# Reordering the work where the stages of a four-layer attention and FFN kernel meet

## The chip, the cores and the metric

The kernel runs on one core of one Trainium2 chip. The metric is the device time of one execution in microseconds (us). Three executions of the kernel before took 1570.99, 1571.07 and 1574.42 us; their median is 1571.07 us.

## The reference

The residual stream `x` is 1024 tokens of 512 numbers. Each of four layers adds an attention of the normalised `x` over a context of 1024 tokens, and then an FFN of the normalised `x`:

```python
x = x + _L0_xattn_ref(_layernorm(x), ctx, Wq, Wk, Wv, Wo)     # 32 heads of 128, 4 KV heads
x = x + _L0_ffn_ref(_layernorm(x), base_W, gate_W, lora_A, lora_B)   # dense + top 2 of 28 experts of rank 8
x = x + _L1_xattn_ref(_layernorm(x), ctx, mask, ...)           # 32 heads, 8 KV heads, RMS norm of q and k
x = x + _L1_ffn_ref(_layernorm(x), W_base, gate_W, A, B)       # dense + top 2 of 8 experts of rank 8
x = x + _L2_xattn_ref(...); x = x + _L2_ffn_ref(...); x = x + _L3_xattn_ref(...); x = x + _L3_ffn_ref(...)
```

The change touches the start, the first two attentions and the first two FFNs. Layers 2 and 3 keep their code.

## The kernel before

**Tiles.** `x` stays in SBUF as 8 tiles of 128 tokens. Every product in float32 is made of three products (`PASSES`) of rounded "high" parts and "low" remainders: ScalarE (ACT) copies a PSUM bank to the high part, and VectorE (DVE) subtracts that from the bank for the low part. For weights, which come by DMA from the SP queue into `stage_q`, `stage_o` and `stage_kv`, the low part of some 512-wide slices is made by GpSimd (POOL, `low`, L488) and of others by VectorE (`low_wq`, L1721).

**Order.** Nothing is scheduled at run time. Each engine works through its own list in the order of the code, and waits on semaphores. So an instruction that waits holds up all behind it on its engine.

**An attention** is a pipeline of 64 steps (8 head groups by 8 tiles). In `attention` of TensorE (L737) step `t` holds the q product of step t+1 (first attention, `q_unit`) or t (second, `q_proj`), the transposes of the probabilities of step t-2 (`p_transpose`, L840), the scores of step t-1 (L759), the output product of step t-3 (`out_proj`, L869, bank psY) and the product with V of step t-2 (`attend`, L850). VectorE's list for a step (L1847 on) holds the layer norm `xn` (`ln_norm`), the low part of the transposed probabilities (`pT_lo`), the row maxima (`row_max`), the low part of q, the division by the sum (`normalise`), the residual addition (`x_add`), the low part of the attended values (`oT_lo`) and the statistics of a finished tile (`last_stats`).

**Where stages meet.** The steps from 60 on (`LN_SLOT`) finish the residual tiles one by one, and each such step also transposes one normalised tile for the FFN (`ln_transpose`, L706; its low part, `ln_lo`, on VectorE). The transposes use the bank psP (psT for tile 7), which the probabilities' transposes use too: `p_transpose(63)` waits until the low part of tile 4 has been read out. Steps 63 and 64 have no q product. Behind the loop an epilogue drains the last steps with `dense_product` 0 and 1 of the FFN among them.

**The FFN** (`ffn_step`, L975 and L2045) makes for each tile a gate product (L720, bank psQ), on VectorE the choice of two experts (`gates`, L1770, which ends in the hidden values `s_sb`), a transpose of those (`hidden_transpose`, L955), the dense product (L733) and the experts' product (L971), the last two in one of three banks (`ring3`). The weights of the experts' product are cut into parts (`high_b`, `low_b`) once the last output product of the attention is done. `hidden_transpose(0)` waits for the low part of tile 6, and tile 7 of the norm is transposed behind `dense_product(2)`.

**The second attention's head.** Its step 0 holds the q product of tile 0, the norm transpose of tile 6, the k and v product (`kv_proj`, L812), the norm transpose of tile 7, the q product of tile 1, and the transposes of q and k; step 1 the k and v product, the scores of step 0, the q product of tile 2 and the transposes. VectorE's step 0 has the low part of tile 7 ahead of `qk_normalise(0)`, which makes `q_sb` (L1892) from a reciprocal root (`rms`) of POOL.

**The start.** SP issues tiles 0 and 1 of `x`, four slices of the first q weights, then the context (1 MB), the first k and v weights (0.5 MB) and the other six tiles of `x` (1.5 MB). POOL makes low parts of two q slices, of two context slices and of the k and v weights, and only then the reciprocal roots of tiles 2 on; VectorE has its share of the context's low parts ahead of the statistics of tile 2.

## Time and profile before

| | us |
|---|---|
| profiled execution, whole | 1570.53 |
| its span, first to last instruction | 1568.7 |
| median of three timed executions | 1571.07 |
| TensorE matmuls busy (PE) | 1501.3 (96%) |
| weight loads busy (PEld) | 1323.4 (84%) |
| VectorE busy (DVE) | 1008.9 (64%) |
| ScalarE busy (ACT) | 821.1 (52%) |
| GpSimd busy (POOL) | 379.4 (24%) |

The span is what lies between the first and the last instruction. Matmuls overlap, so the difference between the starts of two groups tells the time that the first holds TensorE better than its length does. The mean granted TensorE clock was 0.985 of full speed.

### The profile page before, as it was taken

Reading aid. Unit: us, or ns where it says so; the run is one execution under the profiler, and the core shown is the slowest. Engines: PE = TensorE matmul, PEld = TensorE weight load, DVE = VectorE, ACT = ScalarE, POOL = GpSimd, SP = SyncE. Lnnn points to the kernel's source line nnn. Section 1 sums busy time; section 2 is a strip of 40 time slices with the busy share of each in tenths; the row PEclk is TensorE's granted clock in tenths of the full one; section 3 lists DMA queues with packets and bytes.
Section 4 is the critical chain, followed back from the end, with each engine's and each line's share of the span. In section 5 each row is a group of like instructions: output and inputs, shape, how many; then the busy total and the mean of one; then the engine's idle time right before and its main releaser. Section 6 shows DMA issues by size and latency. Waiting matters only on the chain.

```text
span 1568.7 us, 27791 instructions
## 1 busy us (share of the span) xinstructions
PE 1501.3 (96%) x9658; PEld 1323.4 (84%) x9658; DVE 1008.9 (64%) x2475; ACT 821.1 (52%) x2862; POOL 379.4 (24%) x388
## 2 busy tenths in 40 slices
PE   7999999999999998999999999999999998879896
PEld 7899999999999997788888888888888887667785
DVE  6666556655665568766665666656666677688775
ACT  4556445644555455346565556555565652554542
POOL 4102010201111011133232332323232321543420
PEclk9999999999999999999999999999999998799998
DMA  4100100100011001010101010101100001111001
GB/s 182 62 28 28 42 28 28 56 14 28 28 55 36 33 13 41 28 41 28 41 28 41 28 50 19 68 8 62 41 28 32 5 8 55 44 55 35 24 11 57
DMA packets 14624, 60.21 MB, mean 38 GB/s; under 512 B 2085, under 2 KB 3493, under 8 KB 9497
## 3 DMA queue, kind: packets, MB, share of 16 engines
q1 hardware_dynamic: 14488, 58.46, 10.5%
q8 instruction: 79, 1.29, 0.4%
q14 instruction: 57, 0.46, 0.1%
HBM read 56.36 MB, written 2.10 MB: 37 GB/s over the span
## 4 chain that ended last, share of the span: by engine, by line
PE 59%; issue 27%; DVE 7%; POOL 3%; ACT 2%; DMA 1%; POOLq 0%; DVEq 0%; SPq 0%; ACTq 0%
PE psY L869 15%; PE psQ L790 11%; PE psKV L812 8%; PE psSO L759 3%; PE psSO L856 2%; PE psTP L822 2%; PE psQ L775 2%; PE psTP L775 2%; PE psSO L760 2%; POOL wo L488 1%; PE psTP L840 1%; PE psKV L733 1%; PE psQ L1137 1%; PE psQ L720 1%; PE psTP L706 1%
## 5 line engine op out<-in xcount | busy, mean ns | idle before, releaser
L869 PE MATMUL psY<-wo,oT 128*128 128x512 f32 x1536 | 384.9, 399 | 1.8 <-DVE oT L1721 1.2
L869 PEld LDWEIGHTS psY<-wo,oT 128*128 128x128 f32 x1536 | 278.6, 188 | 65.8 <-POOL wo L488 2.2
L488 POOL TENSOR_TENSOR wo<-stage_o,wo 128x512 fp32r<-128x512 f32 (+2 forms) x71 | 91.1, 1309 | 309.0 <-ACT wo L1275 309.0
L1275 ACT ACTIVATE pT<-psTP 128x512 fp32r<-128x512 f32 (+1 forms) x128 | 62.8, 491 | 169.4 <-PE psTP L840 169.4
L593 POOL TENSOR_TENSOR rms<-ms_eps,minus_half 128x5 f32<-128x5 f32 x64 | 74.7, 1168 | 280.2 <-DVE ms_eps L1884 277.2
L1356 ACT ACTIVATE prob<-wide,neg_mx 128x128 f32<-128x128 f32 x256 | 99.8, 391 | 75.0 <-DVE neg_mx L1871 74.8
L1353 ACT ACTIVATE prob<-s_sb,neg_mx 128x64 f32<-128x64 f32 x256 | 86.0, 337 | 98.3 <-DVE neg_mx L1871 98.3
L1721 DVE TENSOR_TENSOR pT<-psTP,pT 128x512 fp32r<-128x512 f32 (+1 forms) x128 | 71.3, 557 | 77.4 <-ACT pT L1275 76.4
L1721 DVE TENSOR_TENSOR v<-psKV,v 128x128 fp32r<-128x128 f32 x64 | 18.7, 292 | 140.4 <-ACT v L1275 140.4
L812 PEld LDWEIGHTS psKV<-wkv,arena 128*128 128x128 f32 x768 | 99.8, 190 | 9.0 <-DVE kT L1908 4.6
L812 PE MATMUL psKV<-wkv,arena 128*128 128x256 f32 x768 | 103.4, 284 | 1.2 <-DVE kT L1908 1.2
L790 PE MATMUL psQ<-wq,hT 128*128 128x512 f32 x384 | 104.0, 408 | 0.0
L775 PE MATMUL psQ<-hT,wq 128*128 128x256 f32 x768 | 99.6, 285 | 4.2 <-DVE hT L1721 2.9
L790 PE MATMUL psQ<-hT 128*128 128x512 f32 x372 | 100.1, 407 | 0.0
L775 PEld LDWEIGHTS psQ<-hT,wq 128*128 128x128 f32 x768 | 94.9, 192 | 5.9 <-DVE hT L1721 3.1
L812 PE MATMUL psKV<-wkv,hT 128*128 128x256 f32 x768 | 99.8, 286 | 0.0
L775 PE MATMUL psTP<-hT,wq 128*128 128x256 f32 x768 | 99.1, 286 | 0.0
L1275 ACT ACTIVATE oT<-psSO 128x512 fp32r<-128x512 f32 (+1 forms) x132 | 76.4, 579 | 38.8 <-PE psY L869 32.1
L775 PEld LDWEIGHTS psTP<-hT,wq 128*128 128x128 f32 x768 | 96.0, 195 | 0.0
L812 PEld LDWEIGHTS psKV<-wkv,hT 128*128 128x128 f32 x768 | 94.1, 192 | 0.3
L1326 ACT ACTIVATE pT<-psQ 128x128 fp32r<-128x128 f32 x252 | 66.3, 280 | 53.4 <-PE psQ L790 53.4
L1721 DVE TENSOR_TENSOR oT<-psSO,oT 128x512 fp32r<-128x512 f32 (+1 forms) x132 | 88.7, 672 | 7.5 <-ACT oT L1275 7.2
(303 smaller groups left out, 3389.5 us busy)
## 6 DMA issues: line engine op xcount, KB each, us to landing
stage_o<-in_wo SPq DMA_DIRECT2D x16, 1024.0 KB, 4.8
stage_q<-in_wq SPq DMA_DIRECT2D x15, 1024.0 KB, 5.3
stage_kv<-in_wkv SPq DMA_DIRECT2D x12, 512.0 KB, 3.6
stage_q<-in_ctx SPq DMA_DIRECT2D x16, 256.0 KB, 2.8
stage_o<-in_ctxT SPq DMA_DIRECT2D x2, 1024.0 KB, 5.8
stage_q<-in_base SPq DMA_DIRECT2D x2, 1024.0 KB, 4.9
out<-x_res SPq DMA_DIRECT2D x8, 256.0 KB, 2.4
x_res<-in_x SPq DMA_DIRECT2D x1, 1536.0 KB, 11.1
```

The lines of the kernel that those rows point to most:

```text
L488: g.tensor_tensor(dst[LO], stage, dst[HI].bitcast(f32), ALU.subtract).then_inc(ld[done or what + "_lo"], 1)
L593: g.tensor_tensor(rms[:, t.res(2)], ms_eps[:, t.res(2)], minus_half[:, 0:5], ALU.pow).then_inc(s["rms"], 1)
L759: mm(bank[:, at:at + 2 * keys], q_of(HI), k_of(slice(0, 2)), start=True, stop=False)
L775: m = mm(out, wq[:, wl, c, head], lat_pair(xl, c, k.res(NT) // 2), start=c == 0 and i == 0, stop=c == KT - 1 and i == 2)
L790: m = mm(by_eight(q_bank(st)[:]), lat(xl, k, n), wq_slice(st.div(NT) + a.wq0, wl, k), start=k == 0 and i == 0, stop=k == KT - 1 and i == 2)
L812: m = mm(psKV[:, b * 256:(b + 1) * 256], lhsT, wkv_k(wl, k, 256), start=k == 0 and i == 0, stop=k == KT - 1 and i == 2)
L869: m = mm(psY[:], oT[:, ol, h, :], wo[:, wl, h, :], start=h == 0 and i == 0, stop=h == HQ - 1 and i == 2)
L1275: copy = lambda o, i: nc.scalar.activation(o, i, ACT.Copy)
L1326: i = nc.scalar.activation(junk_q[h], q_bank(st)[:, h * HD:(h + 1) * HD], ACT.Square, accum_out=ssq[:, n, h:h + 1])
L1353: e = nc.scalar.activation(prob[:, at], s_sb[:, at], ACT.Exp, bias=neg_mx[:, j:j + 1], scale=1.0, accum_out=sums[:, j:j + 1])
L1356: e = nc.scalar.activation(prob[:, at], wide[:, at], ACT.Exp, bias=neg_mx[:, j:j + 1], scale=a.scale, accum_out=sums[:, j:j + 1])
L1721: return V.tensor_tensor(dst_lo, src, dst_hi.bitcast(f32), ALU.subtract)
```

## The change

It moves instructions in the lists of all engines and gives two FFN products other banks. The core of the diff:

```diff
@@ ring3: banks of the dense products
-        return (psS, psKV, psY)[n % 3]
+        return (psKV, psS, psY)[n % 3]
@@ sync: loads at the start
         sp.wait_ge(ld["x1"], 16)
+        sp.dma_start(x[:, 2:4], io["x"][:, 2:4]).then_inc(ld["x23"], 16)
         sp.dma_start(stage_o[:], io["ctxT"][0]).then_inc(ld["ctx_in"], 16)
         sp.dma_start(stage_kv[:], io["wkv0"][0]).then_inc(ld["wkv_in"], 16)
-        sp.dma_start(x[:, 2:NT], io["x"][:, 2:NT]).then_inc(ld["x_rest"], 16)
+        sp.dma_start(x[:, 4:NT], io["x"][:, 4:NT]).then_inc(ld["x_rest"], 16)
@@ gpsimd
         low_wq(0)
+        low("wq", halves(wq, 2), stage_q[:, 2], 3, "wq_lo_v")
         low_ctx(0)
...
             ln_rstd(1, n)
-            if n == 3:
+            if n == 2:
                 low_wq(8)
@@ tensor: scores(u)
+                if a.index == 1 and u.t == 0:
+                    pe.wait_ge(FS["x_add"], NT)
@@ tensor: kv_proj
-                    pe.wait_ge(FS["x_add"], NT)
+                    pe.wait_ge(FS["x_add"], NT - 1)
@@ tensor: attention, the loop over steps
                             q_proj(t, 2, 4)
+                        if t.t == 0:
+                            experts(FF[0], NT - 1)
+                        if t.t == 1:
+                            q_proj(t.back(-1), 0, 4)
                         kv_proj(t)
...
                     if t1.exists and not units:
                         scores(t1)
-                        if not t.exists:
+                        if t.exists:
                             gate_product(f, 0)
+                        else:
+                            dense_product(f, 0)
...
-                if a.norm_slot(t) == "between":
+                if a.rms and a.norm_slot(t) == "between":
                     ln_transpose(next_ln, t.t - LN_SLOT, ...)
                 if a.rms and t2.exists and t.exists:
                     attend(t2)
+                if a.rms and not t.exists:
+                    gate_product(f, 0)
                 if t3.exists:
                     out_proj(t3, 0, 4)
+                if not a.rms and a.norm_slot(t) == "between":
+                    ln_transpose(next_ln, t.t - LN_SLOT, ...)
                 if a.rms and not t.exists:
                     scores(t1)
+                    dense_product(f, 0)
                     attend(t2)
...
                 if a.index == 1 and t.static and t.t == 0:
+                    q_proj(t.back(-1), 0, 4)
                     ln_transpose(2, NT - 1, ...)
                 if t.exists and a.rms:
-                    if t.t < 2:
-                        q_proj(t.back(-1), 0, 4)
                     q_transpose(t)
                     k_transpose(t)
@@ tensor: attention, the epilogue
-            if a.rms:
-                gate_product(f, 0)
-            pe.wait_ge(s["max"], last.c + 1)
-            dense_product(f, 0)
             p_transpose(last)
             out_proj(before, 0, 4)
             attend(last)
+            pe.wait_ge(s["max"], last.c + 1)
+            dense_product(f, 1)
             ln_transpose(next_ln, 5, ...)
-            dense_product(f, 1)
+            gate_product(f, 1)
             out_proj(last, 0, 4)
             ln_transpose(next_ln, 6, ...)
@@ tensor: ffn_step
-            if t == 1:
-                gate_product(f, t)
...
             if t < NT:
+                if t == 1:
+                    ln_transpose(f.ln, NT - 1, lambda: None)
                 if t > 1:
                     gate_product(f, t)
-                if t == 1:
-                    pe.wait_ge(A["x_add"], (f.index + 1) * STEPS)
-                    dense_product(f, 2)
-                    ln_transpose(f.ln, NT - 1, lambda: None)
-                if t > 2:
+                    if t == 2:
+                        pe.wait_ge(A["x_add"], (f.index + 1) * STEPS)
                     dense_product(f, t)
-            if 0 <= u < NT:
+            if 0 <= u < NT - (f.index == 0):
                 experts(f, u)
@@ scalar: first attention, steps 60 on
-                    ln_hi(next_ln, t.t - LN_SLOT)   # ahead of exps(t1)
+                    ln_hi(next_ln, t.t - LN_SLOT)   # behind exps(t1)
-                    next_wq(t)   # step 62, ahead of exps
+                if not a.rms and t.t == STEPS - 2:
+                    next_wq(t)   # step 62, behind oT_hi
-            pT_hi(last)
             gate_exp(FF[a.index], 0)
+            pT_hi(last)
@@ vector: attention
                 if scores_first:
+                    pT_lo(t2)
                     row_max(t1)
                 if a.norm_slot(t):
                     ln_norm(next_ln, t.t - LN_SLOT)
-                if t2.exists:
+                if t2.exists and not scores_first:
                     pT_lo(t2)
...
-                if a.norm_slot(t) == "between":
+                if a.rms and a.norm_slot(t) == "between":
                     ln_lo(next_ln, t.t - LN_SLOT)
...
                     x_add(t3)
+                if not a.rms and a.norm_slot(t) == "between":
+                    ln_lo(next_ln, t.t - LN_SLOT)
...
+                if not a.rms and t.t == STEPS - 2:
+                    low_wq(8)   # was ahead of normalise(t1)
@@ vector: the epilogue and the start
-            pT_lo(last)
             gates(FF[a.index], 0)
             ln_norm(next_ln, 5)
+            pT_lo(last)
...
-        low_wq(0, 2)
         ln_lo(0, 0)
```

## Rows read from the trace of the kernel before

**Rows 1.** The page: the chain of work that ended last, by engine.

```profile
PE 59%; issue 27%; DVE 7%; POOL 3%; ACT 2%; DMA 1%; POOLq 0%; DVEq 0%; SPq 0%; ACTq 0%
```

**Rows 2.** TensorE's waits over the span: releaser, total us, times, longest.

```profile
PE psTP L955 <- DVE s_sb L1778: 4.7, 4, 2.6
...
PE psTP L706 <- DVE pT L1721: 2.3, 3, 1.0
```

**Rows 3.** Windows: stretch, length, busy us by engine, PEclk, DMA share, GB/s.

```profile
10.00:12.00 2.00, 0.01 (x1) 0.01 (x1) 1.94 (x4) 0.99 (x3) 0.09 (x1) 1.00 1.07 447
641.00:660.00 19.00, 16.91 (x102) 14.20 (x101) 15.45 (x52) 8.90 (x17) 4.34 (x5) 1.00 0.15 56
1313.00:1321.00 8.00, 7.60 (x25) 6.44 (x25) 4.64 (x22) 0.63 (x3) 0.81 (x2) 0.50 0.00 1
```

**Rows 4.** Timeline of the start: start, length, engine, line, operation, idle before.

```profile
14.87 2.93 POOL L488 TENSOR_TENSOR wkv<-stage_kv,wkv 128x512 fp32r<-128x512 f32 x2
...
18.96 1.12 PE L706 MATMUL psTP<-ident,xn 128*128 128x128 f32 x4 [3.82 <-DVE xn L1762]
```

**Rows 5.** Timeline of VectorE, one round of the first attention's last steps.

```profile
596.24 0.55 DVE L1762 TENSOR_SCALAR xn<-x_res,mv,rstd 128x512 f32<-128x512 f32 x1 [0.67 <-POOL rstd L501]
...
605.27 0.55 DVE L1762 TENSOR_SCALAR xn<-x_res,mv,rstd 128x512 f32<-128x512 f32 x1 [0.66 <-POOL rstd L501]
```

**Rows 6.** Timeline of TensorE, from step 63 to the last transposes.

```profile
619.00 0.98 PE L850 MATMUL psSO<-pT,arena 128*128 128x256 f32 x6 [1.97 <-DVE pT L1721]
...
626.85 3.00 PE L733 MATMUL psSO<-wq,hT 128*128 128x512 f32 x12
629.69 0.60 PE L840 MATMUL psTP<-ident,prob 128*128 128x128 f32 x4
```

**Rows 7.** Timeline of VectorE, step 64 and the gates behind it.

```profile
622.90 0.69 DVE L1858 TENSOR_TENSOR wide<-psSO,wide 128x512 f32<-128x512 f32 x1
...
626.44 0.69 DVE L1877 TENSOR_TENSOR prob<-prob,rsums 128x512 f32<-128x512 f32 x1
...
631.56 0.18 DVE L1819 MAX8 top<-psQ 128x8 f32<-128x28 f32 x1
...
633.66 0.54 DVE L1762 TENSOR_SCALAR xn<-x_res,mv,rstd 128x512 f32<-128x512 f32 x1
```

**Rows 8.** Timeline of all engines behind the first attention's last product.

```profile
637.51 2.89 PE L869 MATMUL psY<-wo,oT 128*128 128x512 f32 x12
...
640.43 0.69 DVE L1926 TENSOR_TENSOR x_res<-x_res,psY 128x512 f32<-128x512 f32 x1 [2.82 <-PE psY L869]
...
642.85 2.72 POOL L488 TENSOR_TENSOR wo<-stage_o,wo 112x512 fp32r<-112x512 f32 x2
...
642.92 1.50 DVE L1762 TENSOR_SCALAR xn<-x_res,mv,rstd 128x512 f32<-128x512 f32 x1
```

**Rows 9.** Timeline of all engines, head of the second attention.

```profile
693.53 0.68 DVE L1892 TENSOR_TENSOR q_sb<-psQ,rms 128x512 f32<-128x512 f32 x1
...
696.41 1.69 PE L812 MATMUL psKV<-wkv,arena 128*128 128x256 f32 x12 [0.84 <-DVE kT L1908]
...
700.43 0.69 DVE L1892 TENSOR_TENSOR q_sb<-psY,rms 128x512 f32<-128x512 f32 x1
```

**Rows 10.** Timeline of all engines, end of the second attention and its FFN.

```profile
1283.75 0.22 PE L759 MATMUL psSO<-kT,qT 128*128 128x128 f32 x1
...
1289.57 0.68 DVE L1721 TENSOR_TENSOR hT<-psTP,hT 128x512 fp32r<-128x512 f32 x1
...
1290.39 0.41 PE L840 MATMUL psTP<-ident,prob 128*128 128x128 f32 x2 [0.45 <-DVE hT L1721]
...
1303.71 1.50 DVE L1762 TENSOR_SCALAR xn<-x_res,mv,rstd 128x512 f32<-128x512 f32 x1
...
1313.40 0.42 PE L955 MATMUL psTP<-ident,s_sb 128*64 128x128 f32 x1 [2.61 <-DVE s_sb L1778]
...
1316.06 5.42 PE L733 MATMUL psSO<-hT 128*128 128x512 f32 x12
```

More of the change, by code:

```diff
@@ L697, in wq_split @@
         def wq_split(load, k):
-            pe.wait_ge(ld["wq_lo" if k < 2 else "wq_lo_v"], load * 2 + (k % 2 + 1))
+            pe.wait_ge(ld["wq_lo" if k < 2 else "wq_lo_v"], load * 2 + (2 if load == 0 and k > 1 else k % 2 + 1))
         def ln_transpose(ln, n, free):
@@ L916, in attention @@
                     attend(t2)
+                if a.rms and not t.exists:
+                    gate_product(f, 0)
                 if t3.exists:
                     out_proj(t3, 0, 4)
+                if not a.rms and a.norm_slot(t) == "between":
+                    ln_transpose(next_ln, t.t - LN_SLOT, lambda: ln_bank_free(next_ln, t.t - LN_SLOT, t2))
                 if a.rms and not t.exists:
                     scores(t1)
+                    dense_product(f, 0)
                     attend(t2)
@@ L1434, in attention @@
                     next_wq1(t)
-                if t.exists and not a.rms and not early and t.res(8) == 6:
+                if t.exists and not a.rms and not early and t.res(8) == 6 and t.t < LN_SLOT:
                     next_wq(t)
@@ L1472, in attention @@
             last = Step(STEPS - 1, STEPS, done=a.done)
+            gate_exp(FF[a.index], 0)
             pT_hi(last)
-            gate_exp(FF[a.index], 0)
             oT_hi(last)
@@ L1747, in x_stats @@
         def x_stats(n):
-            dve.wait_ge(ld[f"x{n}" if n < 2 else "x_rest"], 16)
+            dve.wait_ge(ld[f"x{n}" if n < 2 else "x23" if n < 4 else "x_rest"], 16)
             ln_stats(0, n)
@@ L1973, in attention @@
                     ln_lo(0, n)
-                if a.norm_slot(t) == "between":
+                if a.rms and a.norm_slot(t) == "between":
                     ln_lo(next_ln, t.t - LN_SLOT)
@@ L1979, in attention @@
                     qk_normalise(t)
-                if t.exists and not a.rms and t.res(8) == 6:
+                if t.exists and not a.rms and t.res(8) == 6 and t.t < LN_SLOT:
                     low_wq(t.div(8) + 1)
@@ L1985, in attention @@
                     x_add(t3)
+                if not a.rms and a.norm_slot(t) == "between":
+                    ln_lo(next_ln, t.t - LN_SLOT)
                 if t2.exists and a.rms:
```

## The prediction

> **What bounds the kernel now.** The chain that ended last, on the page, gives 59% of the span to TensorE's matmuls and 27% to its own issue, 7% to VectorE [rows 1]. So TensorE's list is the time, plus the places where it waits. TensorE's waits say where: no large group stands there, only single waits of 0.4 to 3.8 us; the hidden values of the FFNs, for example, cost 4.7 us in four waits [rows 2]. The timelines of those places then show who is late: nearly always VectorE, at a point of its list where several short results are due one after another. The windows add one thing. From 1313 to 1321 us, in the second FFN, TensorE has half its clock (PEclk 0.50, 1.2 instead of 2.4 GHz), while the same stretch of the first FFN has all of it [rows 3].
>
> All differences below are starts minus starts. A q or dense product holds TensorE for 2.8 us (626.85 to 629.69 [rows 6]), and so does an output product; gate 1.5, scores 1.0, a group of four transposes 0.4, attend 0.7. A copy or subtraction of 512 columns takes 0.6 on ACT and 0.68 on VectorE.
>
> **The start: +1.2.** Tiles 2 and 3 arrive sooner, but their statistics stand in VectorE's list behind the context's low parts, and their root stands in POOL's list behind the low part of the k and v weights: that ends at 14.87 + 2.93 = 17.80, and root, normalising and transposes follow, these at 18.96, after 3.82 us without work for TensorE [rows 4]. The 0.52 MB now ahead of the context cost it 0.52 MB / 447 GB/s = 1.2 us [rows 3]; POOL's context slices, its weights, the root and the transposes go with it. The first q product may start up to 0.6 us sooner, as VectorE loses a slice to POOL, but it only ends in the longer wait. Bounds: 0 (the context is late for nobody) to +2.5 (the third slice delays POOL too). I take 1.2.
>
> **The first attention, steps 60 to 63: -1.3.** Norm transposes no longer wait in front of the output product (2.3 us in three waits [rows 2]). But VectorE goes round its list in 605.27 - 596.24 = 9.03 us per step [rows 5], and TensorE needs only 8.1 (2.9 + 0.4 + 1.0 + 2.8 + 0.4 + 0.7). In the round of before, the low part of the norm (0.68 [rows 10]) lies in the time in which VectorE waits for the exponentials; now it stands behind `x_add` and adds 0.6 to the round, of which some 0.4 comes back from a wait for ACT. At about 9.2 per round the wait moves to the transposes of the probabilities and is not gone: 0. In step 63 the weight slices stand no longer ahead of the exponentials and the division, which have been waiting behind them; the gate product fills the wait for the probabilities (0.9), and `attend`'s wait (1.97 [rows 6]) shrinks, though VectorE now has the two slices right ahead of `pT_lo(61)`. I take -1.3, bounds -5.7 (all the waits of these steps) and 0.
>
> **Step 64 and the epilogue: +4.1.** This is the largest term. From the start of scores(63), new list: scores 1.0, dense product 2.8, then transposes 62, done at 4.4; ACT's copy to 5.0; VectorE's `pT_lo(62)`, which now stands ahead of `row_max(63)`, to 5.7. The row maxima start only then. From their start to the end of the division it is 626.44 + 0.69 - 622.90 = 4.2 us [rows 7]: probabilities at 10.0. Then `x_add` 0.6, `oT_lo` 0.6, and the low part of tile 4 until 11.9. TensorE has done output product 61, attend 62 and transpose 4 by 8.2, and the next in its list is `p_transpose(63)`, which needs both: a wait of 3.7, where before the dense product stood in that place and the transposes started at 629.69 with no wait [rows 6]. Then output product 62 until 15.1; VectorE has statistics (1.0), `gates(0)` and the norm of tile 5 (631.56 to 633.66 and 0.5 [rows 7]), and only then `pT_lo(63)`: ready about 16.1, a wait of 0.9 for `attend(63)`, against 0.5 that goes. 3.7 + 0.4 = 4.1; bounds 2 and 5.
>
> **Behind the last output product: +2.0.** Before, tile 7's normalised values were ready at 642.92 + 1.50 = 644.42, which is 4.2 after the end of the output product's place (637.51 + 2.7), and POOL's expert weights at 642.85 + 2.72 = 645.57, 5.4 after it [rows 8]. Both hang on that product (through `x_add` at 640.43 and ACT), and the new list keeps their order. Between stood gate 1 (1.5) and dense 2 (2.8); now only transposes of 1.0 in all stand ahead of `experts(0)`: 4.4 us of waits, and 0.3 for the next hidden values. In exchange 0.9 goes here and, as dense 2 now stands before `experts(1)`, the 1.8 us of waits at the third hidden transpose. 4.7 - 2.7 = 2.0; bounds 0.5 and 3.5.
>
> One rule bears on this place. The normalising took 1.50 with POOL's subtraction running, against 0.55 alone [rows 5, 8]. The Trainium skill (GPSIMD Engine Reference, Key points) says that POOL shares its SBUF interfaces with VectorE and contends with instructions in a two-port mode or with two SBUF inputs; trace and rule agree. By it the collision comes back in the new order and is now paid by TensorE; if it didn't, the term would be 1.0 smaller.
>
> **Head of the second attention: +2.5.** The expert product of tile 7 behind the q product removes a wait of 0.7. But q product 1 now stands before tile 7's transposes, and VectorE has that tile's low part ahead of `q_sb(0)`: transposes, copy, low part and `q_sb` follow one another (0.6 + 0.7 + 0.7 + 0.7) with nothing left for TensorE, a wait of 2.3; `q_sb(0)`, at 693.53 before [rows 9], comes at about 695. Then q product 2 fills the 0.84 before the k product of step 1, but it is gone from where it covered the other chain: from that k product to `q_sb(1)` ready it is 700.43 + 0.69 - 696.41 = 4.7 us [rows 9], with only 1.5 + 0.8 of work now, a wait of 2.4. The probabilities of step 0 are then late by 1 too. Sum of waits 8.0 against 5.5. Bounds 1 and 3.5.
>
> **Second attention's end and FFN: +2.2 at equal clock.** The same steps. From scores(63) to tile 4's low part it is 1289.57 + 0.68 - 1283.75 = 6.5 [rows 10]; with gate and output product ahead scores start 0.4 later, at 1284.1, so the transposes of the probabilities start at about 1290.7 against 1290.39 before [rows 10], gate and dense product done in both: +0.3. `pT_lo(63)` behind `gates(0)` adds 0.5. Behind the last output product the normalised tile 7 comes late as in the first FFN (1.50 again, 1303.71 [rows 10]), and `gates(1)`, 0.7 longer here than the 2.1 of the first FFN, stands behind it, without gate 1 and dense 2 to cover either: +4.0. The wait of 2.61 at the third hidden transpose goes [rows 10]: net +2.2. Bounds 0 and 4.
>
> **The clock: +3.** In the second FFN half clock made 12 products last 5.42 instead of 3.0 and the gate 1.3 more: 3.8 us [rows 3, 6, 10], after TensorE had worked little for some 5 us. The new order works 1.0 in 5.4 us there in both FFNs. So I take the second FFN as slow as before (0) and the first one, whose clock was 1.00 [rows 3], falling too, with 3.0 for a gate, a dense and an expert product. Bounds -3.8 and +4.5. The Trainium skill (TensorE: Matmul & The Clock Gate, HAM oscillation) says that idle gaps send the engine back to half clock, and every gap costs anew; by it the fall comes wherever the new waits stand, which is the +3; the rival without it stands below.
>
> **Sum.** 1.2 - 1.3 + 4.1 + 2.0 + 2.5 + 2.2 + 3.0 = 13.7. On the profiled execution's 1570.53 (span 1568.7 and 1.8 around it) that is 1584.2; the median shown is 0.5 above that execution. Own range 1578 to 1590.
>
> **Rivals.**
> - *The waits, without the clock.* The first FFN keeps full clock: 1581.2; if the second does too, 3.8 less, 1577.4. For it: step 63 of before waited 3.4 us in 7 and kept 1.00. Against: there longer products stood between. 0.17.
> - *The products fill what they were moved into.* VectorE's results depend on inputs rather than on its list, so gate 0, dense 0 and dense 2 cover the waits of 3.4 in step 63, 1.8 and 2.6 in the FFNs, the half clock (3.8) goes with the last, and nothing new is due: 1570.5 + 1.2 - 11.6 = 1560. It decides at `p_transpose(63)`: if it starts within 1 us of the transposes before it, this holds. Against it: `pT_lo(62)` stands ahead of the row maxima in the new list. 0.13.
> - *Gains and waits cancel.* Steps 60 to 63 give 4 to 5 us instead of 1.3, the head of the second attention nothing, and the clock does as now: 1584.2 - 3 - 2.5 - 3 - 3 = 1573, or two or three lower. 0.15.
>
> **How the numbers follow.** Forecast 0.55, the rivals 0.17, 0.13, 0.15. What a measurement here can tell from no change is 0.3%, 4.7 us: faster is below 1566.4, slower above 1575.8. Faster holds the filling rival, 0.13; within 0.3%, two thirds of the cancelling one, 0.10; slower the rest, 0.77. The range 1567 to 1590 leaves out the filling rival and the worst of the bounds.
>
> **What would show it.** Right: VectorE's rounds in steps 60 to 62 still 9 us or more; 3 us or more of wait before `p_transpose(63)` in the first attention and 2 in the second; TensorE working 1 us in the 5 behind each last output product; PEclk 0.50 in the first FFN; a wait of 2 us before each of the first two q transposes; norm transposes at 20.2 at the start. Wrong: the FFN's first gate started no later than before relative to the work done, or PEclk 1.00 in both FFNs.

## The result and the profile after

The changed kernel takes 1588.12 us (median of four executions, 1585.94 to 1588.55), 17.0 more than the 1571.12 of the kernel before beside it: ratio 1.0108, 95% interval 1.0083 to 1.0118. Its profiled execution took 1588.29 us, with a span of 1586.6 and a mean granted clock of 0.975 (before: 1570.53, 1568.7 and 0.985). The prediction was 1584.2, range 1567 to 1590.

TensorE's waits that are new or have grown [rows 2], then four windows [rows 3]:

```profile
PE psTP L827 <- DVE q_sb L1906: 5.9, 3, 2.3
PE psTP L845 <- DVE hT L1735: 5.8, 3, 3.4
PE psTP L968 <- DVE hT L1735: 4.2, 2, 2.1
```

```profile
641.00:660.00 19.00, 15.24 (x69) 12.54 (x68) 12.19 (x36) 6.34 (x12) 3.75 (x4) 0.82 0.16 56
1320.00:1336.00 16.00, 13.93 (x54) 10.66 (x55) 10.78 (x44) 2.13 (x8) 2.35 (x4) 0.68 0.39 132
700.00:720.00 20.00, 14.10 (x78) 12.08 (x76) 8.72 (x24) 7.25 (x36) 3.08 (x3) 0.83 0.00 2
598.55:607.30 8.75, 8.61 (x61) 7.82 (x60) 6.79 (x14) 4.57 (x15) 0.55 (x1) 1.00 0.20 60
```

The low part of a norm (`hT`), the normalised values and `q_sb` are waited for, all from VectorE; and three stretches run with PEclk (the granted clock as a share of full speed) at 0.82, 0.68 and 0.83. The first of them had 1.00 before. The last row is one round of VectorE: 8.75 us, in which it works for 6.79. The same round before [rows 5]:

```profile
596.24:605.27 9.03, 8.39 (x62) 7.77 (x60) 6.98 (x14) 4.53 (x13) 0.55 (x1) 1.00 0.18 58
```

TensorE's timeline: the transposes of the probabilities, one group per round, then from the norm transposes of step 64 on [rows 6, 8].

```profile
588.59 0.60 PE L845 MATMUL psTP<-ident,prob 128*128 128x128 f32 x4
...
596.73 0.60 PE L845 MATMUL psTP<-ident,prob 128*128 128x128 f32 x4
...
605.18 0.63 PE L845 MATMUL psTP<-ident,prob 128*128 128x128 f32 x4
...
613.93 0.63 PE L845 MATMUL psTP<-ident,prob 128*128 128x128 f32 x4 [0.73 <-DVE hT L1735]
...
627.72 0.66 PE L708 MATMUL psTP<-ident,xn 128*128 128x128 f32 x4
631.76 0.63 PE L845 MATMUL psTP<-ident,prob 128*128 128x128 f32 x4 [3.39 <-DVE hT L1735]
632.15 4.58 PE L874 MATMUL psY<-wo,oT 128*128 128x512 f32 x12
636.57 0.88 PE L855 MATMUL psSO<-pT,arena 128*128 128x256 f32 x6
...
647.29 0.43 PE L968 MATMUL psTP<-ident,s_sb 128*112 128x128 f32 x2 [2.08 <-DVE hT L1735]
648.85 0.66 PE L708 MATMUL psTP<-ident,xn 128*128 128x128 f32 x4 [1.13 <-DVE xn L1776]
650.06 2.90 PE L984 MATMUL psKV<-wo,oT 112*128 112x512 f32 x6 [0.56 <-POOL wo L489]
...
653.04 2.91 PE L722 MATMUL psQ<-wkv,hT 128*128 128x252 f32 x12
```

The rounds are 8.14, 8.45 and 8.75, the last with a wait of 0.73: TensorE runs ahead of VectorE, whose rounds are 8.88 and 8.75, until it has caught up with it. Later the transposes of the last probabilities wait 3.39 with everything that could cover them done, and the output product behind them holds TensorE for 636.57 - 632.15 = 4.42 instead of 2.8: half clock. Behind the last output product come waits of 2.08, 1.13 and 0.56, and an expert product and a gate product that hold TensorE 2.7 each instead of 1.5.

The head of the second attention, and the end of it with its FFN [rows 9, 10]:

```profile
703.21 0.66 PE L827 MATMUL psTP<-ident,q_sb 128*128 128x128 f32 x4 [2.01 <-DVE q_sb L1906]
...
703.73 4.59 PE L795 MATMUL psQ<-hT 128*128 128x512 f32 x12
...
712.81 0.66 PE L827 MATMUL psTP<-ident,q_sb 128*128 128x128 f32 x4 [2.26 <-DVE q_sb L1906]
...
1305.08 0.66 PE L845 MATMUL psTP<-ident,prob 128*128 128x128 f32 x2 [1.70 <-DVE hT L1735]
1305.39 4.42 PE L874 MATMUL psY<-wo,oT 128*128 128x512 f32 x12
...
1327.57 5.20 PE L735 MATMUL psY<-hT 128*128 128x512 f32 x12
```

Both q transposes wait over 2 us, and q product 2 (4.43 to the next) runs mostly at half clock.

To see where the 17.9 us between the spans arise, I cut each trace at six instructions: the transposes of the probabilities of steps 60 and 65 (P60, P65) in the first attention, the last hidden transpose of its FFN (H), the first output product of the second attention (O), its last transposes of probabilities (Q), and the last hidden transpose of the second FFN (G). Each column is a difference of two starts. The kernels below the second row are explained in the sections that follow:

| kernel | start to P60 | P60 to P65 | P65 to H | H to O | O to Q | Q to G | G to end | span |
|---|---|---|---|---|---|---|---|---|
| before | 586.6 | 43.1 | 53.9 | 31.4 | 575.4 | 53.5 | 224.8 | 1568.7 |
| after | 588.6 | 43.2 | 59.4 | 37.7 | 576.2 | 55.3 | 226.2 | 1586.6 |
| start_back | 585.5 | 43.2 | 58.0 | 36.1 | 576.2 | 55.3 | 226.3 | 1580.6 |
| head_back | 586.5 | 43.2 | 59.3 | 31.4 | 576.3 | 54.9 | 229.3 | 1580.9 |
| behind_back | 587.6 | 43.2 | 54.8 | 36.2 | 576.2 | 53.7 | 227.6 | 1579.2 |
| step64_back | 588.6 | 43.6 | 57.7 | 36.2 | 576.3 | 55.4 | 226.2 | 1583.9 |
| fillers | 588.0 | 43.2 | 58.6 | 33.7 | 577.4 | 53.1 | 226.1 | 1580.1 |
| tile4_psT | 588.9 | 41.3 | 60.8 | 36.1 | 574.2 | 57.1 | 226.2 | 1584.7 |
| best1 | 586.1 | 41.3 | 54.0 | 32.5 | 575.4 | 53.0 | 227.9 | 1570.2 |
| best2 | 586.3 | 41.3 | 54.0 | 31.4 | 575.6 | 54.0 | 227.7 | 1570.3 |
| before_fill | 586.4 | 43.1 | 53.8 | 33.0 | 575.5 | 49.9 | 227.6 | 1569.2 |
| best3 | 584.9 | 41.4 | 54.0 | 33.0 | 575.5 | 51.7 | 228.2 | 1568.7 |
| fillers2 | 588.5 | 43.2 | 56.2 | 33.7 | 576.2 | 54.9 | 224.8 | 1577.5 |
| best4 | 586.9 | 41.3 | 54.0 | 32.4 | 575.4 | 49.0 | 226.2 | 1565.2 |

The first and the last column scatter among kernels with the same code there (G to end: 224.8 to 229.3), the others by some tenths where no clock falls. Where it falls they scatter too: with the new head of the second attention H to O is 37.7 in the changed kernel's trace, but 36.1 or 36.2 in start_back, behind_back, step64_back and tile4_psT, whose code there is the same. So a column says more than a median where 1 or 2 us are asked for, but a single trace can be 1.6 us off in a stretch that has half clock.

### The profile page after: what moved, and what is told of

Same layout as the page of the kernel before. It is cut to its first block, busy times and chain, and to the rows that moved or that the text cites. A ratio compares the mean times of both kernels' runs of the same rounds, so it can differ in the third digit from the quotient of the medians.

```text
span 1586.6 us, 27793 instructions
## 1 busy us (share of the span) xinstructions
PE 1515.3 (96%) x9658; PEld 1333.8 (84%) x9658; DVE 1006.4 (63%) x2474; ACT 820.8 (52%) x2862; POOL 381.0 (24%) x389
## 4 chain that ended last, share of the span: by engine, by line
PE 60%; issue 26%; DVE 7%; POOL 4%; ACT 2%; DMA 1%; POOLq 0%; DVEq 0%; SPq 0%; ACTq 0%
PE psY L874 15%; PE psQ L795 11%; PE psKV L817 8%; PE psSO L764 3%; PE psSO L861 2%; PE psTP L827 2%; POOL wo L489 2%; PE psSO L765 2%; PE psQ L780 1%; PE psTP L845 1%; PE psQ L722 1%; PE psTP L780 1%; PE psSO L735 1%; PE psQ L1147 1%; PE psKV L1191 1%
## 5 line engine op out<-in xcount | busy, mean ns | idle before, releaser
L795 PE MATMUL psQ<-hT 128*128 128x512 f32 x372 | 103.3, 417 | 0.0
L1285 ACT ACTIVATE oT<-psSO 128x512 fp32r<-128x512 f32 (+1 forms) x132 | 76.4, 579 | 40.7 <-PE psY L874 32.4
L489 POOL TENSOR_TENSOR wq<-stage_q,wq 128x512 fp32r<-128x512 f32 x35 | 44.8, 1291 | 205.3 <-ACT wq L1285 166.6
```

What stands on the lines that cost most here:

```text
L489: g.tensor_tensor(dst[LO], stage, dst[HI].bitcast(f32), ALU.subtract).then_inc(ld[done or what + "_lo"], 1)
L795: m = mm(by_eight(q_bank(st)[:]), lat(xl, k, n), wq_slice(st.div(NT) + a.wq0, wl, k), start=k == 0 and i == 0, stop=k == KT - 1 and i == 2)
L1285: copy = lambda o, i: nc.scalar.activation(o, i, ACT.Copy)
```

## Undoing one part at a time

Theory: the order leaves TensorE with nothing to do at four places, and each wait costs its length and the half clock behind it. The rival: the waits are the whole of it. Each kernel undoes one part; its median stands against the kernel before on the same chip, and "less" is against the 17.0 of the changed kernel.

**start_back** gives the start its old order (x 2 to 7 behind the context, weight slice 2 on VectorE):

```diff
-        sp.dma_start(x[:, 2:4], io["x"][:, 2:4]).then_inc(ld["x23"], 16)
         sp.dma_start(stage_o[:], io["ctxT"][0]).then_inc(ld["ctx_in"], 16)
```

> The new kernel with the start as before: tiles 2 to 7 of x behind the context, VectorE makes the low part of weight slice 2. Theory (the second load of x delays the context and with it POOL's chain, 1.2 by the prediction, 1.7 to 2.0 by the position of the probabilities' transposes in the two traces): 1588.1 - 1.9 = 1586.2, and those transposes of step 58 at 586.6 again instead of 588.6. Rival (the start's delay is swallowed by later waits): 1588.1, those transposes still near 588.6.

Measured: 1584.98 (1582.43 to 1590.24), 13.9 above before, ratio 1.0097 (1.0079 to 1.0114): about 3 less than the 17.0. P60 at 585.5. The four traces with the old start and nothing added there (before, this one, best1, best2) have P60 at 585.5 to 586.6, the six with the new one (after, head_back, behind_back, step64_back, fillers, tile4_psT) at 586.5 to 588.9; the means are 586.1 and 588.0. The theory holds with 1.9, though the two groups touch (586.5 and 586.6); of the 3 in the median the rest is within its scatter. The start of the new kernel shows the chain:

```profile
17.35 2.94 POOL L489 TENSOR_TENSOR wkv<-stage_kv,wkv 128x512 fp32r<-128x512 f32 x2
...
21.44 1.01 PE L708 MATMUL psTP<-ident,xn 128*128 128x128 f32 x4 [3.08 <-DVE xn L1776]
```

POOL's low parts of the k and v weights start at 17.35 instead of 14.87, and the norm transposes follow at 21.44 instead of 18.96 [rows 4]. With the old start back the transposes are at 19.80, 1.6 sooner. Two things were undone together here, but the traces tell them apart: ACT's first copy of the context, which waits for the transfer, starts at 13.71 in the changed kernel and at 12.06 in start_back, and POOL has waited 2.69 us for ACT when it comes to its context slices. The late context is the cause, not the third weight slice on POOL.

**head_back** undoes the head of the second attention:

```diff
-                        if t.t == 0:
-                            experts(FF[0], NT - 1)
-                        if t.t == 1:
-                            q_proj(t.back(-1), 0, 4)
...
-                    q_proj(t.back(-1), 0, 4)
                     ln_transpose(2, NT - 1, ...)
+                    if t.t < 2:
+                        q_proj(t.back(-1), 0, 4)
                     q_transpose(t)
```

> The new kernel with the head of the second attention as before (expert product of tile 7 in the FFN's own place, q products 1 and 2 ahead of the q transposes). From the FFN's last hidden transpose to output product 4 the two traces differ by 6.3 us. Theory (two waits of 2 us ahead of the q transposes and a third, and TensorE's clock falling to half because of them): 6.3 less, 1581.8, and PEclk near 1.00 from 700 to 720. Rival (the clock falls there by itself, only the waits are due to the order): 2.5 less as predicted, 1585.6, PEclk still near 0.7.

Measured: 1582.66 (1581.49 to 1583.04), 11.6 above before, ratio 1.0072: 5.4 less. H to O is 31.4, exactly as before, against 37.7, and the clock is 1.00 from 700 to 740. TensorE's timeline, the q transposes of steps 0 and 1, with no idle time noted before them:

```profile
700.29 0.60 PE L824 MATMUL psTP<-ident,q_sb 128*128 128x128 f32 x4
...
707.04 0.60 PE L824 MATMUL psTP<-ident,q_sb 128*128 128x128 f32 x4
```

Neither waits. The theory holds, the rival (only 2.5, half clock all the same) falls.

**behind_back** gives gate 1, dense 2 and tile 7's transposes their old order at the head of both FFNs:

```diff
-            gate_product(f, 1)
             out_proj(last, 0, 4)
...
+            if t == 1:
+                gate_product(f, t)
...
+                    dense_product(f, 2)
                     ln_transpose(f.ln, NT - 1, lambda: None)
```

> The new kernel with gate 1, dense 2 and the norm transposes of tile 7 at the head of the two FFNs in their old order, in the new banks. Theory (what covered the late normalised tile 7 and POOL's expert weights is back): first FFN 2.2 of waits and 2.8 of half clock less, second FFN 2.5 less with the wait of 2.6 and the half clock of before back at the third hidden transpose: 7.5 less, 1580.6, PEclk 1.00 in the first FFN. Rival (the clock falls in the first FFN because of the half clock at step 64 just before, or by itself): 4.7 less, 1583.4, PEclk 0.50 somewhere from 640 to 660.

Measured: 1581.29 (1580.34 to 1583.54), 10.3 above before, ratio 1.0068: 6.7 less, between the theory's 7.5 and the rival's 4.7. P65 to H is 54.8 (4.6 less), Q to G 53.7 (1.6 less); the trace also has 1.6 less in the head of the second attention, which this edit doesn't touch. The window of the first FFN:

```profile
641.00:660.00 19.00, 16.91 (x99) 14.13 (x99) 15.68 (x52) 8.31 (x15) 4.33 (x5) 1.00 0.15 56
```

Full clock with the same busy time as before, although the output product behind the last transposes, some 10 us ahead, still ran at half clock (4.42 to the next). So the fall behind the last output product comes from the waits there and not from the one before.

**step64_back** puts dense product 0 back ahead of the transposes of the last probabilities:

```diff
-                        else:
-                            dense_product(f, 0)
...
+            dense_product(f, 0)
             p_transpose(last)
```

> The new kernel with dense product 0 of both FFNs back ahead of the transposes of the last probabilities (VectorE's and ACT's orders stay new). Theory (those transposes wait 3.4 us for tile 4's low part because the product that covered them was moved ahead): the wait is at most 0.5 and the output product behind it has full clock: in the first attention 3.4 + 1.6 less, in the second 1.7 + 1.5 less: 1588.1 - 8 = 1580. Rival (VectorE's order, pT_lo ahead of the row maxima, is the cause; without the dense product in step 64 the chain of scores, maxima and division is only moved forward with TensorE): the wait moves to attend(63) or stays above 2, and 1585 or more remains.

Measured: 1585.06 (1584.33 to 1586.99), 14.0 above before, ratio 1.009: 3 less, not 8. TensorE's timeline, the transposes of steps 64 and 65 with their output products:

```profile
623.61 1.09 PE L845 MATMUL psTP<-ident,prob 128*128 128x128 f32 x4 [2.52 <-DVE hT L1733]
624.35 4.03 PE L874 MATMUL psY<-wo,oT 128*128 128x512 f32 x12
...
632.15 0.63 PE L845 MATMUL psTP<-ident,prob 128*128 128x128 f32 x4
632.53 2.97 PE L874 MATMUL psY<-wo,oT 128*128 128x512 f32 x12
```

The wait of 3.39 is gone and its output product has full clock (2.97), but the transposes of step 64, which dense 0 had covered, now wait 2.52, and the output product behind those runs at half clock (4.03). There is one product for two holes. The theory fails; the rival has the time (1585 or more) and a wait above 2, though the wait moved to the transposes of step 64. Of the 3 less in the median the trace puts only 1.3 into the first attention's end and its FFN (43.6 and 57.7 against 43.2 and 59.4); 1.5 lies in the head of the second attention, whose code is untouched. In the second attention nothing was gained (O to Q 576.3, Q to G 55.4): its transposes still wait, 1.79 us, for the low part of tile 4. Moving dense 0 alone was the wrong cure there too.

## Is it the clock?

**fillers** leaves the order and puts idle products into the waits, the identity times itself, whose result nobody reads (each stands in the timeline as two matmuls, so 14 are x28):

```diff
+            filler(psT, 14)          # mm(bank, ident, ident), 14 times
             p_transpose(last)
...
+                    if t.t < 2:
+                        filler(psO[:, 0], 8)
                     q_transpose(t)
```

> The new kernel with idle products of the identity in the places where TensorE waits, into banks free there: 14 ahead of the transposes of the last probabilities, 8 ahead of the first hidden transpose, 4 ahead of the norm transposes of tile 7, 8 ahead of each of the first two q transposes; nothing else moved. Theory (the waits themselves, by leaving TensorE idle, cost the half clock behind them; half clock costs 1.6 + 2.8 + 3.8 in the first FFN's surroundings and the head of the second attention and 1.5 + 3.8 in the second): the same waits stay in time but PEclk is 1.00 behind them: 8 to 12 less, 1576 to 1580. Rival (the clock falls for another reason, or the fillers delay the work that they stand ahead of): 1588 or up to 2 more, PEclk 0.50 in the same places.

Measured: 1581.94 (1579.04 to 1585.41), 11.2 above before, ratio 1.007 (1.0055 to 1.0085): 6 less. TensorE's timeline, step 65, then the head of the second attention:

```profile
627.67 3.29 PE L705 MATMUL psTP<-ident 128*128 128x128 f32 x28
631.24 0.63 PE L849 MATMUL psTP<-ident,prob 128*128 128x128 f32 x4 [0.28 <-DVE hT L1745]
631.62 3.00 PE L878 MATMUL psY<-wo,oT 128*128 128x512 f32 x12
635.32 0.98 PE L859 MATMUL psSO<-pT,arena 128*128 128x256 f32 x6 [0.70 <-DVE pT L1745]
...
646.14 3.54 PE L705 MATMUL psTP<-ident 128*128 128x128 f32 x16 [2.08 <-DVE hT L1745]
```

```profile
699.72 1.95 PE L705 MATMUL psSO<-ident 128*128 128x128 f32 x16
701.89 0.66 PE L831 MATMUL psTP<-ident,q_sb 128*128 128x128 f32 x4 [0.22 <-DVE q_sb L1916]
...
702.41 2.98 PE L799 MATMUL psQ<-hT 128*128 128x512 f32 x12
```

The transposes come when they came (631.24 after a start 0.5 sooner), but the output product takes 3.00 instead of 4.58. q product 2 takes 2.98 instead of 4.59, but that proves nothing: it took 2.98 to 3.01 in start_back, behind_back, step64_back and tile4_psT too, behind the same unfilled wait of 2.01. What tells is the k and v product behind the wait of 2.26: 1.70 here, 2.76 to 2.93 in all five traces with that wait unfilled. H to O falls from 37.7 to 33.7: of the head's 6.3 over the 31.4 of before, 4.0 was half clock (2.5 in the four other traces of this head) and 2.3 its waits. One group was set wrongly: the eight at 646.14 stand behind the wait of 2.08 instead of in it, run mostly at half clock and hold TensorE for 3.3 us. And the 14 stand in the second attention too, where they last longer than the wait of 1.70: O to Q is 1.2 longer. The theory holds here in kind, the size is short of its 8 to 12.

**before_fill** and **fillers2** do this with both orders, the second with the fillers now ahead of that wait, so that the two can be compared with the clock held:

> The kernel before with nothing moved, but idle products of the identity in the places of its longest waits: 11 more ahead of the first q product and 8 behind it at the start, 7 ahead of the second q transpose of the second attention, 10 ahead of the third hidden transpose of the second FFN, and 5, 12, 6 and 14 in the waits of the stage behind it. Theory (idle stretches cost the half clock that follows them, whatever the work is): of about 14 us that TensorE's work lasts longer at half clock in the trace of before (16 to 24, 1308 to 1323, 1348 to 1368, 1408 to 1416, 1536 to 1540 us) some 10 come back: 1561. Rival (the fillers delay the work and the clock falls elsewhere instead): 1569 to 1573.

> The new kernel with the idle products of before_fill at the start and behind the second FFN, and in its own waits: 14 and 7 ahead of the transposes of the last probabilities, 8 ahead of the first hidden transposes, 4 ahead of tile 7's norm transposes, 8 ahead of the first two q transposes, none longer than the wait. Theory (of the 17 us between the two kernels 8 to 9 are waits and the rest is half clock behind them): 8 to 9 more than before_fill, about 1570; PEclk 1.00 at 632, 652, 704 to 720 and 1320 to 1332 us. Rival (the waits are the whole of it and the clock only a companion): 15 or more above before_fill.

Measured: 1571.68 (1570.82 to 1573.3), 1.4 above before, ratio 1.0009 (1.0 to 1.0018), and 1580.82 (1578.4 to 1581.15), 10.5 above before, ratio 1.0063 (1.005 to 1.0077). The difference between the two orders is 9.1, as the theory had it; without fillers it is 17.0. Without the 1.5 us that before_fill loses to fillers of its own (below) it would be 10.6, so of the 17.0 some 9 to 11 are waits and the rest half clock. The clock is not held everywhere: in the second FFN of fillers2 one dense product still takes 4.59. But before_fill itself gained nothing, 1561 was expected, and the traces say why. Q to G fell from 53.5 to 49.9: the half clock of the second FFN was worth 3.7. The fillers ahead of the second q transpose, where the kernel before waits for nothing (its wait of 1.71 for `q_sb` is at the third), cost 1.5 (H to O). Behind the second FFN full clock did bring time, but one group of fillers took it again. Windows of that stage, the kernel before, then before_fill:

```profile
1348.00:1370.00 22.00, 17.41 (x92) 16.22 (x92) 11.75 (x28) 11.63 (x27) 12.40 (x16) 0.61 0.23 70
```

```profile
1346.00:1368.00 22.00, 18.30 (x148) 16.86 (x147) 14.12 (x35) 13.59 (x32) 13.24 (x19) 1.00 0.22 71
```

PEclk went from 0.61 to 1.00, and yet from G to the next hidden transpose it is 38.5 us in one and 38.7 in the other. The first gate product of that stage shows what happened between, again before, then before_fill (G is at 1343.9 and 1341.6):

```profile
1376.65 1.66 PE L720 MATMUL psSO<-wkv,hT 128*128 128x256 f32 x12
```

```profile
1371.70 3.29 PE L703 MATMUL psKV<-ident 128*128 128x128 f32 x28
1374.75 1.65 PE L724 MATMUL psSO<-wkv,hT 128*128 128x256 f32 x12
```

The gate product comes 32.7 us behind G before, with no wait ahead of it. In before_fill TensorE has reached that place 30.1 us behind G, 2.7 sooner, but there it has 14 idle products to do, which hold it for 3.0, and the gate product comes at 33.1. So half clock cost 2.7 us in this stage as well; the rival, that fillers delay the work, is what made before_fill no faster. best3 and fillers2 hold the same 14 products. No run left out only these.

## Towards a better kernel

**tile4_psT** gives the norm transposes of tile 4 the bank psT, so that the last probabilities don't wait for its low part:

```diff
-            return psT if n == NT - 1 and ln != 7 else psP
+            return psT if n == NT - 1 and ln != 7 or n == 4 and ln in (1, 3) else psP
```

> The new kernel with the norm transposes of tile 4 in the bank psT in both attentions, so that the transposes of the last probabilities no longer wait for that tile's low part; order unchanged. Theory (the wait of 3.4 us is made half by the shared bank: division done at 629.8, the low part of tile 4 at 631.6): transposes at 629.9 instead of 631.8 after the same start, the wait 1.6; 1.0 to 1.3 of it comes back before attend(63), whose low part stands behind gates(0); with the clock behind a shorter wait staying up, 2 to 4 less in all: 1584 to 1586. Rival (the chain scores, maxima, division alone is the wait): nothing, 1588.

Measured: 1591.31 (1585.81 to 1592.02), 20.5 above before, ratio 1.0123: a miss; 3 more than the changed kernel instead of 2 to 4 less.

```profile
630.18 0.66 PE L846 MATMUL psTP<-ident,prob 128*128 128x128 f32 x4 [1.51 <-DVE prob L1892]
631.38 3.02 PE L875 MATMUL psY<-wo,oT 128*128 128x512 f32 x12 [0.54 <-DVE oT L1736]
636.16 0.98 PE L856 MATMUL psSO<-pT,arena 128*128 128x256 f32 x6 [1.75 <-DVE pT L1736]
636.97 4.50 PE L735 MATMUL psSO<-wq,hT 128*128 128x512 f32 x12
```

The bank was half of the wait, as said (P60 to P65 1.9 less), but 1.4 of it comes back by H: 0.54 for the attended values of step 62 (`oT`), 1.75 for `pT_lo(63)` behind `gates(0)`, and then the half clock, which only moved to the dense product (4.50). The profiled execution is one of the two short ones of five (1586.51, span 1.9 less than the changed kernel's); why the other three took 1591 to 1592 no trace shows.

**best1** takes the kernel before with steps 60 to 64 of the first attention new, tile 4 in psT, and `pT_lo(63)` ahead of the gates:

```diff
+            pT_lo(last)
             gates(FF[a.index], 0)
             ln_norm(next_ln, 5)
-            pT_lo(last)
```

> The kernel before with only the steps 60 to 64 of the first attention new: norm transposes behind the output product, gate product 0 in step 63, dense product 0 in step 64, the weight slices behind the attended values of step 62; tile 4's norm in psT; pT_lo(63) ahead of the gates; start, heads, FFNs and the second attention as before. Theory (steps 60 to 63 gain 3.7, the wait ahead of the last probabilities' transposes is 1.6 to 1.9 instead of 0): 1.8 less than the kernel before, 1569.2. Rival (the clock falls behind that wait as in the new kernel, or the second FFN's chance moves): 0 to 2 more than the kernel before, 1571 to 1573.

Measured: 1572.05 (1570.57 to 1573.6), ratio 1.0006 (0.9998 to 1.0015). P60 to P65 is 41.3, the gain of 1.8 is there, and `attend(63)` waits no more; it is given back by the head (32.5) and the last stages (227.9), whose code is that of before. In the head the third q transpose waits 1.71 in both, and PEclk falls behind it in best1 and not in before. The median shows no gain: the rival's case.

**best2** also splits dense product 2 of the second FFN:

```diff
-                    dense_product(f, 2)
+                    dense_product(f, 2, 0, 2)
...
+                if t == 2 and f.index == 1:
+                    dense_product(f, 2, 2, KT)
```

> As the one before, and in the second FFN the second half of dense product 2 stands behind the gate product, ahead of expert product 1, instead of both halves together. Theory (the half clock of the second FFN comes from the wait of 2.3 to 2.6 at the third hidden transpose; split in two waits of about 1.3, it keeps full clock): 3.8 less than the one before, 1565.4, PEclk 1.00 throughout the second FFN. Rival (the waits are only divided and the clock falls all the same, since the work between them is as little): 1569.

Measured: 1571.61 (1567.78 to 1573.82), ratio 1.0001. Q to G is 54.0, 1.0 more than in best1: the rival's half clock, 3 us above its time. One wait of 1.49 is left, and TensorE has half clock from the gate product behind it (2.65 instead of 1.50) to the end of dense product 3:

```profile
1305.66 0.30 PE L961 MATMUL psTP<-ident,s_sb 128*64 128x128 f32 x1 [1.49 <-DVE s_sb L1790]
...
1315.27 4.97 PE L733 MATMUL psKV<-hT 128*128 128x512 f32 x12
```

**best3** is best1 with all fillers of before_fill:

> The first attention's steps 60 to 64 new as in best1, and the idle products of before_fill. Theory: best1 was 2.1 less than before up to the end of the first FFN and gave it back to half clock later; with the clock held the 2 are kept: 2 less than before_fill, 1559. Rival (VectorE is the bound there and the 2 us are lost at the next wait): the same as before_fill.

Measured: 1569.47 (1565.73 to 1573.22), ratio 0.9993 (0.9983 to 1.0003): not told from before, 2.2 below before_fill: the 2 us are kept, as the theory had it, but not the time of 1559. Here the clock fell twice in the second FFN, once among the fillers and once where none stand:

```profile
1308.25 4.06 PE L703 MATMUL psTP<-ident 128*128 128x128 f32 x20
...
1333.66 0.30 PE L967 MATMUL psTP<-ident,s_sb 128*64 128x128 f32 x1 [0.51 <-DVE s_sb L1804]
...
1335.09 4.58 PE L737 MATMUL psSO<-hT 128*128 128x512 f32 x12
```

**best4** keeps the fillers of the start (11 and 8) and of the second FFN (10 ahead of the third hidden transpose, and 3 new ones ahead of the first). Those of the start show no gain in the table (P60 at 586.4, 584.9 and 586.9 in before_fill, best3 and best4, 585.5 to 586.6 with the old start and no fillers):

```diff
+                if t == 3 and f.index == 1:
+                    pe.wait_ge(LNS[f.ln]["lo"], ln_at(f.ln, NT))
+                    filler(psT, 10)
                 hidden_transpose(f, u)
```

> best1 with idle products only where they helped in the traces so far: the start, and in the second FFN 3 ahead of the first hidden transpose and 10 ahead of the third; none in the head of the second attention (there they delayed the second q transpose by 1.5 us) and none behind the second FFN (there half clock cost nothing, 38.5 us to the next mark against 38.7 with full clock). Theory (2.1 us of the first attention and some 3.7 of the second FFN's half clock are both kept): 3 to 5 less than the kernel before, 1566 to 1567. Rival (what is gained ahead of the last stages is given back in them, as best1 and before_fill showed): 1569 to 1571.

Measured: 1567.07 (1564.19 to 1570.0, 11 executions) against 1571.18 beside it, ratio 0.9971 (0.9962 to 0.998): 4.1 us faster than before, 21 than the changed kernel.

```profile
1309.54 2.50 PE L703 MATMUL psTP<-ident 128*128 128x128 f32 x20
...
1313.63 3.03 PE L737 MATMUL psKV<-hT 128*128 128x512 f32 x12
```

Q to G is 49.0 against 53.5, P60 to P65 41.3 against 43.1; dense 3 has full clock (3.03, where before had 5.42 [rows 10]). 1.0 is lost in the head of the second attention (32.4), half clock behind the wait of 1.71 as in best1. No run has one of these parts alone, so their shares come from the columns only; and the stage behind the second FFN, where half clock costs 2.7, was left without fillers.

## Why the prediction was right, step by step

- *Start*: +1.2 predicted, +2.0 in the trace, 1.9 between the means of the traces. Right in mechanism: the context came 1.6 later than in start_back, and everything behind it; the norm transposes are at 21.44, where the forecast said 20.2, partly by scatter: ACT's second copy starts at 8.52, and at 8.29 in start_back with the old start, against 7.31 before.
- *Steps 60 to 63*: -1.3 predicted, -3.7 measured up to output product 61 (35.49 from P60 instead of 36.34, with dense 0 done as well, 2.8). The step that failed: "at about 9.2 per round the wait moves to the transposes". I took VectorE's 9.03 as its own need; it is busy for 6.98 of that. In the new order it has 6.79 in 8.75 and its waits for ACT's copies are gone, and TensorE, no longer held ahead of the output product, goes round in 8.14 and 8.45 before it meets VectorE's pace. The wait did move to the transposes, as said, but only in the third round and with 0.73. The forecast's own sign, rounds of 9 us or more, is not met.
- *Step 64 and epilogue*: +4.1 predicted, +4.6 measured, of which 1.6 half clock and 3.0 waits. The wait ahead of the last transposes was put at 3.7 and is 3.39; the 0.9 for `pT_lo(63)` did not show, since the output product lasted long enough to hide it. With the clock held it appears, 0.70 (fillers). step64_back and tile4_psT show that this wait has two causes, VectorE's chain and the shared bank, and that no move of one product removes both holes.
- *Behind the last output product*: +2.0 predicted, +2.2 of waits by the starts. The new waits of the profile, 2.08, 1.13 and 0.56, are 3.8 against the 4.7 forecast, and what goes, 0.68 and 1.34, is 2.0 against 2.7. The normalising took 1.49 beside POOL's subtraction, and TensorE waited for it. The Trainium skill (GPSIMD Engine Reference, Key points) names contention of POOL with VectorE's instructions in a two-port mode or with two SBUF inputs. Whether this one is of that kind no run shows, and none took POOL's work away.
- *Head of the second attention*: +2.5 predicted, +2.3 of waits (fillers) and 4.0 of half clock (2.5 in four other traces).
- *Second attention's end and FFN*: +2.2 predicted, +0.8 (O to Q) and +1.8 (Q to G) are 2.6. That is near for a reason the term did not have: the wait ahead of the last transposes is 1.70 and not 2 or more, and the output product behind it ran at half clock (4.34 to the next instead of 2.9, so 1.4), which it did not do in head_back and behind_back.
- *Clock*: +3.0 predicted, 2.8 measured where I put it. What failed is "the first one [FFN] falling too" as the only place: it fell at step 64 (1.6) and in the head (4.0) as well, behind single waits of 3.39, 2.01 and 2.26. The Trainium skill (TensorE: Matmul & The Clock Gate, HAM oscillation) describes a kernel in which every gap costs anew. These places agree with it, the wait of 1.71 that kept full clock in most kernels does not. I used it for one place of three.
- The rest, +1.4 behind G, lies inside the scatter of that stretch, so it can't be called an effect of the change.

The terms read from the traces are 2.0 - 3.7 + 4.6 + 5.0 - 0.3 + 6.3 + 2.6 + 1.4 = 17.9 us, the difference of the spans; -0.3 is what the rest of the first FFN gave back. The two large misses had opposite signs, -2.4 in steps 60 to 63 and +5.4 of clock, so the sum came out nearer than its terms: that part is luck. The rival that the moved products fill their new places is refuted by 3.39 at its own point of decision. The cancelling rival had steps 60 to 63 nearly right (4 to 5 less) and the head, at nothing, wrong. "The waits, without the clock" gave 1581.2, and fillers2, the nearest to that case, takes 1580.82; so close an agreement is chance too, since fillers2 has fillers at the start and behind the second FFN as well, and still one dense product at half clock.

## What to carry to other kernels

A product moved forward to fill a wait leaves its old place open: before moving it, ask what it covered there, and count what arrives last behind it. Price a wait of TensorE by its length and by the half clock of the work behind it, at every place where the wait is new, and test that with products nobody needs. They paid where they stood inside a wait; ahead of work that did not wait they cost what they took (1.5 and 3.0 us), and that can hide what the clock gives back. So compare starts at several marks before calling half clock free. An engine's round time is not its need: take its busy time in the round, and ask which of its waits the new order removes, before calling it the bound.

## What the runs showed of the hardware beyond that

- The granted clock fell to half behind the wait of 3.39 at step 65 in all four traces that have it, and behind the 2.26 in the head in all five, also behind 2.52 in step64_back; it stayed at full behind 1.97 in step 63 of before. With those two waits of the changed order filled with identity products it stayed at full in fillers and fillers2.
- The same code and the same wait gave both: behind the 1.71 at the third q transpose the clock was full in before, best2, best3 and head_back and half in best1 and best4; behind the 2.01 in the head it was half in one trace of five; behind the 1.70 ahead of the second attention's last transposes it was half in the changed kernel and start_back and full in head_back and behind_back.
- Fillers did not always hold it: in best3 twenty matmuls of them took 4.06 us instead of 2.50, though the same twenty kept full clock in best4 and before_fill. Later a dense product took 4.58 behind a wait of 0.51, though TensorE was busy for all of the 20 us from 1313 to 1333. No filler stands there, and in best1, which has none at all, the same product took 4.60 behind 0.56; in before, best2, best4 and before_fill it kept full clock behind 0.52 to 0.55. What decides this stays open.
- The traces differ by up to 4.5 us in the last 225 us, whose code is the same. A gain of 2 us ahead of them can't be read from a few executions; eleven of best1 did not show it.
